# High and low part of x in buffers of three slots for a head, with the sums of x in the third slot

## What is computed

```python
def _L0_cond_ref(x, adapter_ids, base_weight, base_bias, lora_A_w, lora_B_w):
    result = jnp.einsum('bsd,od->bso', x, base_weight) + base_bias
    A, Bw = lora_A_w[adapter_ids], lora_B_w[adapter_ids]
    h = jnp.einsum('bsd,brd->bsr', x, A)
    return result + jnp.einsum('bsr,bor->bso', h, Bw)

def _L1_cond_ref(u, log_dt, C, log_A_real, A_imag, D, length):
    K = _get_kernel(log_dt, C, log_A_real, A_imag, L)     # one filter of 1024 taps for each of 64 heads
    y = irfft(rfft(u, n=2 * L) * rfft(K, n=2 * L))[..., :L]
    y = y + u * D[:, None]
    return y * mask[:, None, :]

x = x + _L0_cond_ref(x, itok_B_6_15, ...)                 # x: 128 x 64 x 1024, float32
x = x + _L1_cond_ref(x, ..., itok_B_78_3631)
```

## Time and profile before

| | before |
|---|---|
| median of 3 runs | 1069.84 us (1069.52 to 1070.04) |
| the profiled execution | 1069.73 us |
| its span, first to last instruction | 1068.0 us |
| TensorE busy | 1061.2 us, 99% |
| VectorE busy | 848.5 us, 79% |
| ScalarE busy | 717.0 us, 67% |
| granted TensorE clock | 1.000 |

### The profile page before, as it was taken

One profiled execution on the slowest core, in us unless ns is written; L12 is line 12 of the kernel. 1 busy time (PEld: TensorE's weight loads), 2 busy tenths in 40 slices (PEclk: granted clock), 3 DMA queues, 4 the chain that ended last, 5 costly groups with the idle time before them and its releaser, 6 DMA issues.

```text
span 1068.0 us, 21568 instructions
## 1 busy us (share of the span) xinstructions
PE 1061.2 (99%) x8088; PEld 1028.8 (96%) x8088; DVE 848.5 (79%) x1263; ACT 717.0 (67%) x1260; POOL 28.6 (3%) x79
## 2 busy tenths in 40 slices
PE   9999999999999999999999999999999999999998
PEld 7999999999999999999999999999989999999997
DVE  7899887878698787878778787877488888888886
ACT  5755545755747466556557467465598888888885
POOL 0000000000000000000000000000010000000000
PEclk9999999999999999999999999999999999999999
DMA  8586758688786978868785888858798978798873
GB/s 290 202 304 221 275 191 284 199 300 307 226 269 211 298 225 277 282 229 275 229 308 179 296 260 259 293 194 283 264 346 286 350 287 335 294 326 317 304 263 123
DMA packets 162586, 284.62 MB, mean 266 GB/s; under 512 B 10739, under 2 KB 125620, under 8 KB 149044
## 3 DMA queue, kind: packets, MB, share of 16 engines
q1 hardware_dynamic: 162484, 283.26, 77.1%
HBM read 193.96 MB, written 89.26 MB: 265 GB/s over the span
## 4 chain that ended last, share of the span: by engine, by line
PE 97%; DVE 1%; ACT 1%; DMA 0%; issue 0%; DVEq 0%; SPq 0%; ACTq 0%
PE acc L1810 37%; PE acc L1970 25%; PE acc L1816 18%; PE acc L1738 5%; PE acc L1782 5%; PE acc L2005 3%; PE acc L1748 2%; DMA x_raw<-x_t 0%; PE acc L1915 0%; ACT x_hi L687 0%; PE acc L1774 0%; DVE x_sb L1262 0%; ACT L845 0%; ACT L851 0%; DVE g_sb L1460 0%
## 5 line engine op out<-in xcount | busy, mean ns | idle before, releaser
L1970 PE MATMUL acc<-u_hi,f_hi 128*128 128x512 f32 (+1 forms) x320 | 128.9, 403 | 0.0
L687 ACT ACTIVATE acc<-acc 128x512 f32<-128x512 f32 x93 | 54.0, 581 | 109.4 <-PE acc L1816 109.3
L1810 PE MATMUL acc<-t_hi,v_lo 128*128 128x256 f32 x512 | 123.0, 279 | 0.0
L1810 PE MATMUL acc<-t_hi,v_hi 128*128 128x256 f32 x512 | 122.9, 279 | 0.0
L1810 PE MATMUL acc<-t_hi,w_pair 128*128 128x256 f32 x960 | 122.4, 279 | 0.0
L1970 PE MATMUL acc<-u_lo,f_hi 128*128 128x512 f32 (+1 forms) x320 | 118.4, 370 | 0.0
L1970 PE MATMUL acc<-u_hi,f_lo 128*128 128x512 f32 (+1 forms) x320 | 118.2, 369 | 0.0
L1810 PEld LDWEIGHTS acc<-t_hi,w_pair 128*128 128x128 f32 x960 | 116.9, 188 | 0.0
L687 ACT ACTIVATE t_hi<-t_raw 128x1024 fp32r<-128x1024 f32 x64 | 67.9, 1061 | 61.7 <-DVE t_raw L1220 33.0
L1105 DVE TENSOR_TENSOR t_lo<-t_raw,t_hi 128x1024 fp32r<-128x1024 f32 x64 | 78.3, 1223 | 34.3 <-ACT t_hi L687 33.9
L1810 PEld LDWEIGHTS acc<-t_hi,v_lo 128*128 128x128 f32 x512 | 96.2, 188 | 0.0
(11 more groups left out here) (205 smaller groups left out, 2673.3 us busy)
## 6 DMA issues: line engine op xcount, KB each, us to landing
w_pair<-weight_scratch SPq DMA_DIRECT2D x71, 1024.0 KB, 6.5
x_scratch<-x_sb SPq DMA_DIRECT2D x32, 1024.0 KB, 6.0
out<-out_sb SPq DMA_DIRECT2D x63, 512.0 KB, 4.8
x_raw<-x_t SPq DMA_DIRECT2D x15, 2048.0 KB, 11.1
u_raw<-x_scratch SPq DMA_DIRECT2D x14, 2048.0 KB, 11.8
wq_raw<-state_scratch SPq DMA_DIRECT2D x16, 1024.0 KB, 8.1
a_raw<-lora_a SPq DMA_DIRECT2D x128, 64.0 KB, 5.7
b_raw<-lora_b SPq DMA_DIRECT2D x128, 64.0 KB, 2.1
```

What stands on the lines that cost most here:

```text
L687: return act.activation(dst, src, ACT.Copy)
L1810: pe.matmul(by_row(bank_part(bank, i)), w[:, k, i, :], hi[:, k, :, :], start=opens and i == 0 and k == 0 and s == 0, stop=False, skip_grou ...
L1970: mm = pe.matmul(bank, w, m, start=first and i == 0, stop=last and i == 2, skip_group_check=onto_closed)
```

## The change

`x_hi` and `x_lo` become `xt_hi` and `xt_lo`, of shape `[P, NT, heads, 3, GH]` with GH = 4: for each head 12 words, of which slots 0 and 1 hold x and slot 2 a sum. Row tiles 0 to 3 (rows 0) and 4 to 7 (rows 1) each hold one sum at a time. T1 and T2 have their high part in rows 0 and T3 and T4 in rows 1; of the low parts T2 and T4 are in rows 0 and T3 in rows 1. T1's low part has a buffer of its own, `t1_lo`, in which its words stand without a gap. The memory is 52 KB a partition for these buffers, as before. `u_raw` 1 and 2 and the second `wq_raw` lie elsewhere over them, and SP's wait ahead of `load_u(1, LAST)` becomes `m_p5[1]`. The zeros that pad the filters' scratch move to `zb`, and the wait for their store (`st_pad`) goes from ScalarE's first T2 to VectorE's `even_sums`. No instruction is added or removed.

```diff
-    x_hi = place("x_hi", [P, NT, N], F32R)
-    x_lo = place("x_lo", [P, NT, N], F32R)
+    XT_SLOTS, T_SLOT = 3, 2
+    xt_shape = [P, NT, heads, XT_SLOTS, GH]
+    xt_hi = place("xt_hi", xt_shape, F32R)
+    xt_lo = place("xt_lo", xt_shape, F32R)
+    xt_raw = place("xt_raw", xt_shape, F32, at=lo_at)
+    XT_HALF = HALF * heads * XT_SLOTS * GH * 4
-    t_lo = place("t_lo", [P, HALF, heads, 3, GH], F32R)
-    t_hi = place("t_hi", [P, HALF, heads, 2, GH], F32R)
+    t1_lo = place("t1_lo", [P, HALF, heads, GH], F32R)
-    LO_SLOT = {"T1": 2, "T2": 0, "T3": 1, "T4": 0}
-    HI_SLOT = {"T1": 0, "T2": 0, "T3": 1, "T4": 1}
+    LO_ROWS = {"T2": 0, "T3": 1, "T4": 0}
+    HI_ROWS = {"T1": 0, "T2": 0, "T3": 1, "T4": 1}
...
-    u_raw = [... enumerate((x_raw_at, x_hi_at, x_lo_at))]
+    u_raw = [... enumerate((x_raw_at, lo_at + XT_HALF, hi_at + XT_HALF))]
-    wq_raw = [..., place("wq_raw1", [P, HQ, BLOCKS, P], F32, at=t_at)]
+    wq_raw = [..., place("wq_raw1", [P, HQ, BLOCKS, P], F32, at=hi_at)]
...
+    def x_row(xt, t):
+        return xt[:, t, :, 0:T_SLOT, :]
+    def x_part(xt, r, c):
+        return xt[:, r * HALF:(r + 1) * HALF, :, c, :]
+    def t_rows(xt, r):
+        return xt[:, r * HALF:(r + 1) * HALF, :, T_SLOT, :]
+    def t_hi(n):
+        return t_rows(xt_hi, HI_ROWS[n])
+    def t_lo(n):
+        return t1_lo[:, :, :, :] if n == "T1" else t_rows(xt_lo, LO_ROWS[n])
...
-                for p in range(2):
-                    sp.wait_ge(m_p3[p], turns(p, g))
+                sp.wait_ge(m_p5[1], n_groups)
                 load_u(1, LAST)
                 store_x1(g, 0)
...
-                copy(x_hi[:, t, :], x_raw[:, t, :]).then_inc(c_xhi, 1)
+                copy(x_row(xt_hi, t), by_column(x_raw[:, t, :])).then_inc(c_xhi, 1)
...
-                product_hi(bank, w_hi, w_lo, block(x_hi, r, c), opens)
-                return product_lo(bank, w_hi, block(x_lo, r, c))
+                product_hi(bank, w_hi, w_lo, x_part(xt_hi, r, c), opens)
+                return product_lo(bank, w_hi, x_part(xt_lo, r, c))
```

More of the change, by code:

```diff
@@ L155, in lora_s4d_kernel @@
     x_raw = place("x_raw", [P, NT, N], F32)
-    x_hi_at = cursor[0]
-    x_hi = place("x_hi", [P, NT, N], F32R)
-    x_lo_at = cursor[0]
-    x_lo = place("x_lo", [P, NT, N], F32R)
-    t_at = cursor[0]
-    t_lo = place("t_lo", [P, HALF, heads, 3, GH], F32R)
-    t_raw = place("t_raw", [P, HALF, heads, 3, GH], F32, at=t_at)
-    t_hi_at = cursor[0]
-    t_hi = place("t_hi", [P, HALF, heads, 2, GH], F32R)
-    t4_raw = place("t4_raw", [P, NT, N], F32, at=x_lo_at)
+    XT_SLOTS, T_SLOT = 3, 2
+    xt_shape = [P, NT, heads, XT_SLOTS, GH]
+    hi_at = cursor[0]
+    xt_hi = place("xt_hi", xt_shape, F32R)
+    lo_at = cursor[0]
+    xt_lo = place("xt_lo", xt_shape, F32R)
+    xt_raw = place("xt_raw", xt_shape, F32, at=lo_at)
+    XT_HALF = HALF * heads * XT_SLOTS * GH * 4
+    t_at = cursor[0]
+    t1_lo = place("t1_lo", [P, HALF, heads, GH], F32R)
+    t1_raw = place("t1_raw", [P, HALF, heads, GH], F32, at=t_at)
     v_shape = [P, HALF, QT, P]
@@ L170, in lora_s4d_kernel @@
     s4_even = place("s4_even", v_shape, F32, at=ge_at)
-    zeros = place("zeros", [heads, KPAD], F32, at=t_hi_at)
+    zeros = place("zeros", [heads, KPAD], F32, at=zb_at)
     T_NAMES = ("T1", "T2", "T3", "T4")
-    LO_SLOT = {"T1": 2, "T2": 0, "T3": 1, "T4": 0}
-    HI_SLOT = {"T1": 0, "T2": 0, "T3": 1, "T4": 1}
+    LO_ROWS = {"T2": 0, "T3": 1, "T4": 0}
+    HI_ROWS = {"T1": 0, "T2": 0, "T3": 1, "T4": 1}
     x1_at = cursor[0]
@@ L194, in lora_s4d_kernel @@
     OUT_EARLY = 2
-    u_raw = [place(f"u_raw{i}", u_shape, F32, at=at) for i, at in enumerate((x_raw_at, x_hi_at, x_lo_at))]
+    u_raw = [place(f"u_raw{i}", u_shape, F32, at=at) for i, at in enumerate((x_raw_at, lo_at + XT_HALF, hi_at + XT_HALF))]
     cursor[0] = fg_at
-    wq_raw = [place("wq_raw0", [P, HQ, BLOCKS, P], F32), place("wq_raw1", [P, HQ, BLOCKS, P], F32, at=t_at)]
+    wq_raw = [place("wq_raw0", [P, HQ, BLOCKS, P], F32), place("wq_raw1", [P, HQ, BLOCKS, P], F32, at=hi_at)]
     out_sb = [place(f"out_sb{i}", [P, 2, n_groups, W8], F32) for i in range(OUT_EARLY)]
@@ L302, in block, with x_half, by_column @@
         return t[:, r * HALF:(r + 1) * HALF, :].rearrange("p k (h a b) -> p k h a b", a=2, b=GH)[:, :, :, c, :]
+    def x_row(xt, t):
+        return xt[:, t, :, 0:T_SLOT, :]
+    def x_part(xt, r, c):
+        return xt[:, r * HALF:(r + 1) * HALF, :, c, :]
+    def x_half(xt, t, c):
+        return xt[:, t, :, c, :]
+    def t_rows(xt, r):
[4 more added lines that the diff above has]
+        return t1_lo[:, :, :, :] if n == "T1" else t_rows(xt_lo, LO_ROWS[n])
+    def by_column(ap):
+        return ap.rearrange("p (h a b) -> p h a b", a=2, b=GH)
     def half(t, c):
@@ L318, in t_source @@
     def t_source(g, n):
-        return block(t4_raw, 0, 1) if n == "T4" else t_raw[:, :, :, LO_SLOT[n], :]
+        if n == "T1":
+            return t1_raw[:, :, :, :]
+        return x_part(xt_raw, 0, 1) if n == "T4" else t_rows(xt_raw, LO_ROWS[n])
     def bank_part(bank, i):
@@ L746, in split_t @@
                     act.wait_ge(m_p5[1] if n == "T2" else m_p4[1], g)
-                if g == 0 and n == "T2":
-                    act.wait_ge(st_pad, 16)
-                copy(t_hi[:, :, :, HI_SLOT[n], :], t_source(g, n)).then_inc(c_thi[n], 1)
+                copy(t_hi(n), t_source(g, n)).then_inc(c_thi[n], 1)
             def split_a(g):
@@ L1180, in even_sums @@
                 dve.wait_ge(ld_e, 16 * 4)
+                dve.wait_ge(st_pad, 16)
                 even_sum(s1, a21, a22, ALU.add, 1)
@@ L1200, in split_x @@
                 dve.wait_ge(c_xhi, NT * g + t + 1)
-                minus_hi(x_lo[:, t, :], x_raw[:, t, :], x_hi[:, t, :]).then_inc(c_xlo, 1)
+                minus_hi(x_row(xt_lo, t), by_column(x_raw[:, t, :]), x_row(xt_hi, t)).then_inc(c_xlo, 1)
             def x_block(r, c):
@@ L1229, in split_t @@
                 dve.wait_ge(c_thi[n], g + 1)
-                minus_hi(t_lo[:, :, :, LO_SLOT[n], :], t_source(g, n),
-                         t_hi[:, :, :, HI_SLOT[n], :]).then_inc(c_tlo[n], 1)
+                minus_hi(t_lo(n), t_source(g, n), t_hi(n)).then_inc(c_tlo[n], 1)
             def split_a(g):
@@ L1736, in adapters_down @@
                         pe.wait_ge(c_xlo, NT * g + t + 1)
-                        for i, m in enumerate((x_hi, x_lo)):
+                        for i, xt in enumerate((xt_hi, xt_lo)):
                             mm = pe.matmul(half(acc[:, H_BANK, :], c),
                                            a_st[:, t, c, :, :].rearrange("p k r -> p (k r)"),
-                                           half(m[:, t, :], c), start=t == 0 and i == 0, stop=t == NT - 1 and i == 1)
+                                           x_half(xt, t, c), start=t == 0 and i == 0, stop=t == NT - 1 and i == 1)
                     mm.then_inc(m_h, 1)
@@ L1745, in plain_products @@
                 c, kk = divmod(k, HALF)
-                pairs = products([w_pair[:, 2 * r + c, s, kk, ii, :] for s in range(2)], (x_hi[:, k, :], x_lo[:, k, :]))
+                pairs = products([w_pair[:, 2 * r + c, s, kk, ii, :] for s in range(2)], (x_row(xt_hi, k), x_row(xt_lo, k)))
                 for s, (w, m) in enumerate(pairs):
-                    mm = pe.matmul(acc[:, plain_bank(i), :], w, m, start=k == 0 and s == 0, stop=False)
+                    mm = pe.matmul(by_column(acc[:, plain_bank(i), :]), w, m, start=k == 0 and s == 0, stop=False)
                 return mm
@@ L1827, in t_product @@
                 pe.wait_ge(c_thi[n], g + 1)
-                product_hi(bank, w_hi, w_lo, t_hi[:, :, :, HI_SLOT[n], :], opens)
+                product_hi(bank, w_hi, w_lo, t_hi(n), opens)
                 pe.wait_ge(c_tlo[n], g + 1)
-                return product_lo(bank, w_hi, t_lo[:, :, :, LO_SLOT[n], :])
+                return product_lo(bank, w_hi, t_lo(n))
             def p1(p, g):
```

## The result

| | before | changed |
|---|---|---|
| median of 12 runs | 1069.76 us (1068.98 to 1070.53) | 1066.95 us (1065.42 to 1068.84) |
| the profiled execution | 1069.73 us | 1065.42 us |
| its span | 1068.0 us | 1063.9 us |

The ratio is 0.9973, with a 95% interval of 0.9964 to 0.9982: 2.9 us less, with the interval from 1.9 to 3.9. The changed kernel's runs scatter over 3.4 us, those of before over 1.6, and the profiled execution is the fastest of the twelve. Three of the twelve have a mean granted clock of 0.998 instead of 0.999 or 1.000, and they take 1067.3, 1068.7 and 1068.8 us, against a median of 1066.5 for the other nine. Experiment 4 has a trace of such an execution.

The account below looks back on a forecast made before the run. TensorE's matmul intervals were taken as the bound. Savings of 3.6, 0.9, 0.9, 0.8 and 0.2 us less costs of 0.9 and 1.1 gave 4.4 us less, 1065.3 us, range 1060.7 to 1070.2 us for 8 in 10.

Parts of the forecast that it names:

- x in p1 and p2, slot 0 of 3: TensorE's reads of x in p1 and p2: 2.772 us a product against 2.83, 3.6 us less.
- p3: TensorE's reads of x in p3: 2.772 us a product against 2.80, 0.9 us less.
- adapters_down: First-stage matmuls of adapters_down: 115.5 ns against 117.2 for 512 matmuls, 0.9 us less.
- all the sums together: Reads of T1 to T4: high parts 0.8 and 0.2 us less, low parts 0.9 and 1.1 us more.
- T1's low reads without gaps: T1's low part in p5: 121.3 ns a read, 4.6 above 116.7, 1.1 us more over 248 matmuls.
- The reason that I gave for slots: TensorE's reads: first of two slots dearer by some 1 ns, third of three by 1.2 ns, at 116.7 against 115.5.
- SP's moved wait: Load of heads 4 to 7 issued some 16 us later, at the stages' border: taken as hidden, no cost.
- the spare bandwidth: DMA queues between 764 and 780 us: 118 GB/s spare over 16 us, 1.9 MB, just the load's size.
- My sum by bytes: Filters of heads 4 to 7: 1920 KB ahead at 381 GB/s push them back 5.2 us, to 782.3.
- my sign of being wrong: At the stages' border: a wait of ScalarE for `u_raw` or `wq_raw` between 775 and 790 us.
- my rival of late loads: Head 4's filters land at 790.7 us, 8.8 us late, and ScalarE then TensorE stand: 1074.1 us; chance 0.08.
- the no-change rival: High-part reads in `product_hi` gain nothing from the wider step: 1069.8 us, no change; chance 0.18.

Follow-up runs that it names:

- Experiment 4: The changed kernel with the sum in slot 0 and x in slots 1 and 2: 1065.72 us, ratio 0.9956 to the kernel before.
- experiments 2 and 3: Kernel before with later load and only high parts in the three-slot buffer: 1068.97 us, ratio 0.9996; with only low parts there: 1073.03 us, ratio 1.0030.
- experiments 4 to 6: First the changed kernel with the sum in slot 0, 1065.72 us; then two kernels of matmuls alone on zeros, varying step and slot, then start addresses.
- experiment 1: The kernel before with only SP's wait ahead of the load of heads 4 to 7 moved to the end of p5: 1072.29 us, ratio 1.0027.
- Experiment 7: The changed kernel with the load of heads 4 to 7 in two halves, the first issued after p7: 1065.03 us, ratio 0.9957 to the kernel before.
- experiment 9: The changed kernel with sum in slot 0, load in halves and filters of heads 4 to 7 ahead of the second half: 1063.82 us, ratio 0.9946.

## Why the prediction came out as it did

The direction and the range were right, and 2.9 us came where 4.4 were forecast. Three terms were off: the reads gained more than forecast, and two costs that I had put at nothing were not nothing. That the time came out within 1.7 us of the forecast is partly luck, since these errors ran against each other.

**The reads, too small.** The step "x in p1 and p2, slot 0 of 3", 3.6 us, was mis-sized. It measured (2.828 - 2.735) x 15 + (2.827 - 2.720) x 47 = 6.4 us. I took 115.5 ns from `t_lo`'s runs of 8, which stand behind 16 reads of another step, and experiments 2 and 3 show that such a mixture costs 1 to 3.5 ns. In the changed kernel p1 and p2, with one step and slot 0 throughout, settle at 113.3. The other terms were near: p3 0.9 forecast and 0.9 measured, adapters_down 0.9 and 1.0, all the sums together 1.0 lost and 0.4 measured. T1's low reads without gaps take 119 to 120 ns against 121.3. The matmuls' total was 7.9 us less instead of 4.4. The reason that I gave for slots, that each has its price, was falsified by experiments 4 to 6, though its numbers held for p3 and for the sums.

**The waits, taken as nothing.** Of the 7.9, the first stage shows 5.7. Counted over the groups from adapters_down in group 1 on, intervals of over 130 ns, less 117 each, make 3.0 us before (25 of them) and 4.8 after (30). That is 1.8 us more. TensorE's waits name the seeds of its banks on ScalarE, 0.9 us against 0.6 before, and `w_pair` loads, 0.7 against nothing. It closes the sum within 0.4 us but was not tried by itself.

**SP's moved wait, the step that failed.** "I take it as hidden" cost 2.9 us, as experiment 1 shows: as much as the whole net gain. Two things were wrong in it. The first is the spare bandwidth. I set 263 GB/s against 381, but the engines can be full at less:

```profile
764.00:780.00 16.00, 16.00 (x87) 14.03 (x86) 11.86 (x18) 14.55 (x38) 1.45 (x3) 1.00 0.99 300
```

In the changed kernel the DMA engines are busy 99% of this stretch at 300 GB/s. Against 263 before that leaves 37 GB/s, which over 16 us is an estimate of 0.6 MB and not 1.9, while between 744 and 758 us they fell from 92% busy to 35%. My sum by bytes was near: it put the filters of head 4 at 782.3 us, and in experiment 1 they landed at 783.2. The second is that I looked at head 4 alone. The filters of head 8 landed at 802.2 us in experiment 1 against 796.7 before, and TensorE stood 1.5 us for them after 1.2 us at head 4. In the changed kernel's profile ScalarE waits 0.2 us for the filters of head 4 and 2.3 us, up to 795.5 us, for those of head 8. So nearly all of the wait lies outside the 775 to 790 us where my sign of being wrong looked for it. The cost is less than my rival of late loads had it (8.8 us).

I also left out that SP's own list is held. With the load, the store and the first filter load issued, SP stood in that filter load's issue for 6.6 us, and all behind it came 5 us later. In all eight traces with the later load or its later half the longest held issue of those that began between 758 and 770 us ended within 0.1 us of the landing of that load. Whether the held list costs time by itself, or only goes along with full DMA engines, these runs don't separate. Experiment 7 sends half the load while the engines are little used, and experiment 9 changes the order of the same bytes.

**What held.** High reads gain in the layout with the wider step, by 1.9 to 3.6 ns even with the low reads left as they were, so the no-change rival falls; the rule of the Trainium skill that reads within one 16-byte line run at full performance ("Advanced Engine Details and Errata", "SBUF Cachelines") does not tell these cases apart, and 113.3, 118.7 and 160.0 ns for the same runs of 4 words at steps 12, 4 and 24 show that the distance matters. Reads without gaps are not the dearest of all, as I had it: matmuls alone took 120.0 at step 8, slot 1. VectorE and ScalarE write with gaps at no cost: `xt_lo` of 1024 elements takes 1222 ns against the earlier trace rows, and ScalarE's copies of 512 elements of x take 624 ns in both kernels. The account closes: 5.7 us less in the first stage by the trace, less 2.9 for the later load by experiment 1, is 2.8 against 2.9 measured.

**Open.** Which property of the two address streams and of the entry sets the steady interval is not settled. 16 blocks gave no period. So it isn't shown either why p1 and p2 gained, only that they did, and by how much. What lets the granted clock fall after one wait of TensorE and not after another is open as well.

## What to carry to other kernels

Where TensorE is the bound, the step between the runs that it reads is worth trying, best over whole products, high and low parts alike, and the price is to be read in place, since it hangs on what runs ahead. An edit of a buffer's layout moves the point from which a load may be issued: look at how busy the DMA engines are in the stretch that the load moves into, at all that stands behind it in the list, and at the later users too. When a median scatters more than before while the profile looks good, compare the mean granted clocks of the executions: here those with 0.998 took some 2 us longer than the others, and the one trace of such an execution has the fall of the clock right behind a wait of TensorE.

## What was not expected of the hardware

- 256 columns read in runs of 4 words take 113.3 to 120.0 ns at steps up to 12, 123.3 at step 16 (slot 0) and 160.0 at step 24, all at a granted clock of 1.00. Reads without gaps are not the cheapest.
- The same instructions on the same addresses run at 113.3 or 116.7 ns a read in matmuls alone. In the whole kernel of experiment 4 the high parts of T2 and T3 (p = 1) take 113.3 ns a read in 14 of 16 turns and 117.8 in two.
- SP was held 3.7 to 6.8 us in the issue of a DMA, until the `u_raw` load ahead of it had landed; in the changed kernel some 3.5 MB were issued by then.
- Behind 2.03 us without work TensorE's granted clock fell to 0.50 for 3.4 us in one execution; behind 2.60 us at the same point in another kernel it did not.
